# Sums of squares in column tiles of 32 tokens, routed sums kept transposed, and two of four squares on VectorE

## The chip, the cores and the metric

The kernel runs on one core of a Trainium2 chip. The metric is the device time of one execution in microseconds, as the median of several runs. TensorE (PE) multiplies, with its weight loads shown beside it as PEld; VectorE (DVE), ScalarE (ACT) and GpSimd (POOL) do the rest; SyncE (SP) issues the transfers.

## What is computed

A small vision tower of two layers over 64 images of 64 tokens, 256 wide. Layer 0 is a patch embedding, sparse attention and a mixture of experts; layer 1 is attention with a polynomial in place of the softmax, and a ternary feed-forward block with two norms. The parts that matter here, from the reference:

```python
att = polymax(where(causal, q @ k.T / 4, -inf))  # x>0: x*x+1; -100<=x<=0: 1-0.01*x; all over 1000
h = h + (att @ v) @ W_proj
# feed-forward of layer 1
x_norm = x / (rms(x) + EPS)
g = gelu(x_norm @ ternary(w_up).T)               # 256 -> 1024
h = h + (g / (rms(g) + EPS)) @ ternary(w_down).T # 1024 -> 256
```

The mean of the squares of g over its 1024 features is needed for each token. The routed part of layer 0's experts is computed for its nonzero rows: one-hot matrices send rows of a table through gates, and their sums over rows (an array of 64 slots by 128 hidden units) go through the experts' last matrix at the end.

## The kernel before, in words

512 tokens (8 images, 4 tiles of 128 tokens) make a slot, and there are 8 slots. A first half (up to 492 us) runs layer 0 for all slots. The second half, where the change lies, runs layer 1 slot by slot; VectorE, ScalarE and TensorE each go through their own list of work in a written order (the three functions `slot_B`), and semaphores join them. Slots 1 to 4 are trips of a loop and carry a batch of the routed rows each, slot 5 the last routed step, slots 6 and 7 none. Next to slot g's second half runs the first half of slot g + 1.

In a slot TensorE's order is: scores of tiles 2 and 3 (`B2_scores`, L623 and L629); the Gram products of the slot before (`gram`, L675); values of tiles 0 and 1 (L643); the downward products of the slot before for tiles 0 and 1 (`B3_down`, L687); a projection (L652); downward products of tiles 2 and 3; transposes (L322); the routed sums (`routed_sums`, L546) and the turn of the one-hots (L557); the keys and queries of the next slot (L332); values and projection of the other pair; routed gates (L567); the next slot's v (`B1_v`, L609); transposes; scores of the next slot's tiles 0 and 1; and the upward products (`B3_up`, L665).

An upward product of chunk f (of NF = 8 chunks of 128 features) fills a PSUM bank of 512 tokens. ScalarE takes it out through the gelu (L930, semaphore g_ok), makes a 16-bit high half of it (L932, gh_out), and VectorE subtracts to give the low half (`g_parts`, L1558, gl_out). Banks 4, 6, 7, 5 take turns, so that chunk f waits for the gelu of chunk f - 4. Between the gelus ScalarE does `relus` (L910), `quads` (the squares of the polynomial, L920) and `lins` (L915) of the next slot's tiles 0 and 1; `poly` on VectorE (L1501, L1507) waits for them.

The sum of squares of a token is the diagonal of a Gram matrix. `gram(g, f)` multiplies, for each tile of 128 tokens, the high half by the high and low halves: 4 matmuls of 128 by 128 weights and 256 columns for each f, collected over f in banks 6 and 7. All 8 chunks come after the scores of tile 3 (GRAM_LAG = NF). `mean_squares` on VectorE (L1565) multiplies each 128 by 256 block by a mask (1 on the diagonal of the first half, 2 on that of the second) and sums a row. The downward products use banks 6 and 7 too, and so wait for it (msq_ok). In the last slot `B3_down_last` alternates gram(f) and the 8 downward matmuls of f.

`routed_sums` multiplies 16 times 128 by 64 one-hot weights (f32) with 128 columns of gated rows, into 64 partitions; `sums_in` (L1439) adds them to racc. In slot 5 `gated_sums` multiplies racc by a transposed table, TensorE turns the product and ScalarE copies it out for `routed_out` (L579). The first slot's `quads` run on ScalarE while VectorE chooses the experts (`expert_choice`, which calls `first_polys` in the middle).

## Time and profile before

| | us |
|---|---|
| median of 3 runs | 953.96 (951.94 to 956.42) |
| the profiled execution | 949.92 |
| its span | 948.0 |
| TensorE busy | 775.9 (82% of the span) |
| VectorE busy | 655.9 (69%) |
| ScalarE busy | 390.5 (41%) |
| mean granted clock of TensorE | 0.916 |

The span is the time from the first to the last recorded instruction of the profiled execution; the rest of its 949.92 us lies around it. A granted clock of 1.0 is 2.4 GHz and 0.5 is 1.2 GHz. An engine that is busy for less than the whole span can still set the time of a stage, so the stages have to be read one by one. A matrix product in f32 leaves two pairs of records (weight load and matmul), one in f16 leaves one. Matmuls overlap: a record says 0.27 us where the next one begins 0.1 us later, so that paces are taken from start to start.

### The profile page before, as it was taken

Reading aid. Unit: us, or ns where it says so; the run is one execution under the profiler, and the core shown is the slowest. Engines: PE = TensorE matmul, PEld = TensorE weight load, DVE = VectorE, ACT = ScalarE, POOL = GpSimd, SP = SyncE. Lnnn points to the kernel's source line nnn. Section 1 sums busy time; section 2 is a strip of 40 time slices with the busy share of each in tenths; the row PEclk is TensorE's granted clock in tenths of the full one; section 3 lists DMA queues with packets and bytes.
Section 4 is the critical chain, followed back from the end, with each engine's and each line's share of the span. In section 5 each row is a group of like instructions: output and inputs, shape, how many; then the busy total and the mean of one; then the engine's idle time right before and its main releaser. Section 6 shows DMA issues by size and latency. Waiting matters only on the chain.

```text
span 948.0 us, 23223 instructions
## 1 busy us (share of the span) xinstructions
PE 775.9 (82%) x9703; PEld 544.6 (57%) x9703; DVE 655.9 (69%) x1471; ACT 390.5 (41%) x552; POOL 114.4 (12%) x76
## 2 busy tenths in 40 slices
PE   3669788897979788897678779999898989899956
PEld 2446465655546564655447448577575757575634
DVE  6457778586776858688768648596868678383742
ACT  3233332423333232333233274664839283554622
POOL 0030211312030031210001001010100001010000
PEclk9969999999999999998595689999999999998968
DMA  8051010201001010020000000000000000000000
GB/s 296 1 174 48 1 66 0 66 0 66 0 2 65 0 66 0 0 88 1 1 1 1 2 1 6 20 0 22 0 22 0 22 1 24 2 1 24 2 23 23
DMA packets 6779, 26.97 MB, mean 28 GB/s; under 512 B 2256, under 2 KB 3152, under 8 KB 5072
## 3 DMA queue, kind: packets, MB, share of 16 engines
q1 hardware_dynamic: 6736, 26.35, 7.5%
q8 instruction: 33, 0.54, 0.2%
q14 instruction: 10, 0.08, 0.0%
HBM read 22.15 MB, written 4.19 MB: 28 GB/s over the span
## 4 chain that ended last, share of the span: by engine, by line
PE 40%; issue 24%; DVE 22%; ACT 7%; POOL 6%; DMA 1%; DVEq 0%; POOLq 0%; SPq 0%; ACTq 0%
PE PS L304 8%; PE PS L687 5%; PE PS L332 5%; PE PS L652 3%; POOL w_s L1021 3%; PE PS L629 3%; PE PS L322 3%; DVE kM L1155 2%; PE PS L675 2%; PE PS L430 2%; PE PS L665 2%; PE PS L546 2%; DVE xn L1124 2%; PE PS L623 2%; POOL rstd L1005 2%
## 5 line engine op out<-in xcount | busy, mean ns | idle before, releaser
L304 PE MATMUL PS<-tokW_h,w_s 128*128 128x256 f16 x576 | 72.2, 289 | 27.0 <-DVE w_s L1299 16.4
L665 PE MATMUL PS<-xT,wqkv_h 128*128 128x512 f16 x256 | 70.8, 431 | 23.9 <-ACT w_s L930 22.1
L811 ACT ACTIVATE Pm<-Pm 128x1024 f32<-128x1024 f32 x32 | 33.9, 1058 | 135.5 <-DVE Pm L1225 135.5
L304 PEld LDWEIGHTS PS<-tokW_h,w_s 128*128 128x128 f16 x576 | 58.4, 103 | 38.1 <-issue 28.4
L1005 POOL TENSOR_TENSOR rstd<-ve,mhalf 128x4 f32<-128x4 f32 x24 | 28.0, 1168 | 363.1 <-DVE ve L1120 363.1
L1558 DVE TENSOR_TENSOR work<-w_s,work 128x512 f16<-128x512 f32 x48 | 32.5, 690 | 47.5 <-ACT work L932 47.5
L665 PEld LDWEIGHTS PS<-xT,wqkv_h 128*128 128x128 f16 x256 | 25.2, 107 | 64.5 <-ACT w_s L930 32.5
L322 PE MATMUL PS<-ident_s,xn 128*128 128x128 f32 x256 | 45.6, 303 | 15.6 <-DVE xn L1124 14.9
L818 ACT ACTIVATE PT<-PS 128x512 f32<-128x512 f32 x64 | 37.6, 595 | 44.0 <-PE PS L420 43.8
L332 PE MATMUL PS<-xT,wat_h 128*128 128x512 f16 x192 | 48.5, 415 | 7.6 <-DVE xT L1494 7.6
L1021 POOL TENSOR_TENSOR w_s<-work,w_s 128x1536 f16<-128x1536 f32 x14 | 43.1, 3102 | 94.0 <-ACT w_s L842 94.0
L687 PE MATMUL PS<-tokW_h,work 128*128 128x256 f16 x448 | 51.3, 273 | 0.5 <-DVE msq L1565 0.5
L420 PE MATMUL PS<-ident_s,Pm 128*128 128x128 f32 x256 | 44.7, 310 | 8.1 <-ACT Pm L811 4.6
L687 PEld LDWEIGHTS PS<-tokW_h,work 128*128 128x128 f16 x448 | 43.3, 98 | 7.0 <-DVE msq L1565 0.7
L1112 DVE BATCH_NORM_STATS2 st<-H 128x6 f32 (+1 forms) x128 | 45.6, 413 | 2.0 <-DVE H L1519 0.5
L430 PE MATMUL PS<-vbuf,PT 128*64 128x34 f32 x1024 | 42.7, 236 | 4.8 <-ACT PT L818 4.7
L322 PEld LDWEIGHTS PS<-ident_s,xn 128*128 128x128 f32 x256 | 31.3, 150 | 26.4 <-DVE xn L1124 17.2
L1124 DVE TENSOR_SCALAR xn<-H,mv,rstd 128x256 f32 (+1 forms) x96 | 33.1, 407 | 19.2 <-POOL rstd L1005 19.2
L1234 DVE RECIPROCAL rden<-PS 128x16 f32<-128x16 f32 x32 | 8.2, 256 | 55.1 <-PE PS L430 55.1
L430 PEld LDWEIGHTS PS<-vbuf,PT 128*64 128x64 f32 x1024 | 37.2, 149 | 14.9 <-ACT PT L818 7.7
L408 PE MATMUL PS<-mb,selb 128*128 128x256 bf16 x128 | 22.5, 305 | 26.7 <-DVE Pm L1225 20.3
L652 PE MATMUL PS<-wpr_s,xT 128*128 128x256 f32 x128 | 34.8, 419 | 11.2 <-DVE xT L1512 11.2
(237 smaller groups left out, 1672.8 us busy)
## 6 DMA issues: line engine op xcount, KB each, us to landing
work<-in_x SPq DMA_DIRECT2D x8, 1536.0 KB, 6.4
out<-H SPq DMA_DIRECT2D x8, 512.0 KB, 2.6
w_s<-in_w SPq DMA_DIRECT2D x3, 1024.0 KB, 6.8
wup_s<-in_wup SPq DMA_DIRECT2D x1, 1024.0 KB, 5.2
wdn_s<-in_wdn SPq DMA_DIRECT2D x1, 1024.0 KB, 7.2
w_s<-in_tokW SPq DMA_DIRECT2D x1, 768.0 KB, 7.5
wup_s<-in_wqkv SPq DMA_DIRECT2D x1, 768.0 KB, 8.1
wdn_s<-in_s SPq DMA_DIRECT2D x3, 256.0 KB, 6.1
```

The source lines that it names most:

```text
L304: m = pe.matmul(dst, halves_[xi][:, k, rows], w[:, wi, k, cols], start=(n == 0), stop=(n == 3 * chunks - 1))
L322: m = pe.transpose(PS[:, bank, t * P:(t + 1) * P], xn[:, t, c * P:(c + 1) * P], ident_s[:, :])
L332: m = pe.matmul(PS[0:cols, bank, :], w[:, wi, c, col:col + cols], x[xi][:, c, 0:TOK], start=(n == 0), stop=(n == 3 * C - 1))
L420: m = pe.transpose(PS[:, 4 + half, hp * P:(hp + 1) * P], Pm[:, t % 2, at:at + P], ident_s[:, :])
L430: m = pe.matmul(PS[b * L:(b + 1) * L, 6 + t % 2, hp * 2 * VW:(hp + 1) * 2 * VW], PT[:, t % 2, hp, b * L:(b + 1) * L], Vb[:, 2 * t + b, hp, ...
L652: m = pe.matmul(PS[:, bank, (t % 2) * E:(t % 2 + 1) * E], xT2[:, c, t * P:(t + 1) * P], wpr_s[:, c, :], start=(c == 0), stop=(c == C - 1))
L665: m = pe.matmul(PS[:, UP_BANKS[f % 4], :], wup_h[:, c, f * P:(f + 1) * P], part[:, c, :], start=(k == 0), stop=(k == 2 * C - 1))
L687: m = pe.matmul(PS[:, 6 + t // 2, (t % 2) * E:(t % 2 + 1) * E], part[:, f, t * P:(t + 1) * P], wdn_h[:, f, :], start=(k == 0), stop=(k == ...
L1005: pool.tensor_tensor(dst[:, :], src[:, :], mhalf[:, :], ALU.pow).then_inc(done, 1)
L1021: pool.tensor_tensor(p_lo[:, ks, :], patch[:, ks, :], p_hi[:, ks, :], ALU.subtract)\
L1112: dve.bn_stats(st_[:, t, :], H[:, TILES * g + t, :]).then_inc(in_st, 1)
L1124: dve.tensor_scalar(xn[:, t, :], H[:, TILES * g + t, :], mv_[:, t, 0:1], scale[:, t:t + 1], ALU.subtract, ALU.mult).then_inc(done, 1)
```

## The change

- `gram`: a tile of 128 tokens becomes four column tiles of 32 tokens. Each is a matmul with 32 columns of weights and 64 moving columns (32 high, 32 low), placed in its own 32 columns of the array; 16 matmuls for each f in place of 4, all collected in 256 columns of bank 6. The masks and the outputs of `mean_squares` shrink to 128 by 64, and it waits for one semaphore count a slot.
- GRAM_LAG becomes 4: the Gram products of chunks 0 to 3 are issued within `B3_up`, each after the upward product four chunks later; chunks 4 to 7 stay behind the scores.
- Bank 6 is no longer an upward bank: three banks (4, 7, 5) take turns, and chunk f waits for the gelu of chunk f - 3. The downward products of tiles 0 and 1 go to bank 7 and no longer wait for the mean squares; those of tiles 2 and 3 go to bank 6 and wait for all four. Queries swap banks 6 and 7.
- `quads` of tiles 0 and 1 leave ScalarE: VectorE multiplies (`v_quads`), ahead of `g_parts` in every slot and in `first_polys`. Those of tiles 2 and 3 stay on ScalarE.
- ScalarE issues the high half of chunk f behind the gelu of chunk f + 1 (and, for the first two, behind `lins`).
- `routed_sums` swaps its operands: weights are the 128 by 128 gated rows, the moving side the 64 one-hot columns; the result, and racc, are the transposed array of 128 by 64. `gated_sums` gives gT at once; one transpose and one copy go at the start (tabC), and another transpose with its copy in slot 5.

Left out of the diff below are renamed semaphores, the banks in `a_B1_q` and `ffn_out`, and the removed lines of `routed_tables`.

```diff
@@ -147,9 +147,9 @@
         PH = PS[:, 0:2, :].rearrange("p b n -> p (b n)").bitcast(F16)
-        racc = sb("racc", [64, HID]); gm = sb("gm", [64, HID]); gT = sb("gT", [P, 64])
-        UP_BANKS = (4, 6, 7, 5)
-        GRAM_LAG = NF
+        racc = sb("racc", [P, 64]); gT = sb("gT", [P, 64])
+        UP_BANKS = (4, 7, 5)
+        GRAM_LAG = 4
...
@@ -187,8 +187,8 @@
         lin = (u, late)
-        diag = PT[:, 0, 0:2, :].rearrange("p k n -> p (k n)")
-        diag_out = PT[:, 1, :, :].rearrange("p (t k) n -> p t (k n)", t=TILES)
+        diag = PT[:, 0, 0, 0:64]
+        diag_out = PT[:, 1, 0:TILES, 0:64]
...
@@ -543,7 +542,7 @@
                 for k in range(RB):
-                    m = pe.matmul(PS[0:64, 2, 0:HID], one_hot_w[:, k, :], wz_k[:, k, :],
+                    m = pe.matmul(PS[:, 2, 0:64], wz_k[:, k, :], one_hot_w[:, k, :],
...
@@ -572,8 +571,6 @@
-                pe.wait_ge(gm_ok, 1)
-                pe.transpose(PS[:, 0, 0:64], gm[:, :], ident_s[0:64, 0:64]).then_inc(gT_mm, 1)
...
@@ -590,9 +587,9 @@
                         pe.wait_ge(h5_ok, TILES * (g - 2) + 2 * c + 2)
-                    elif not first(g) and c == 1:
+                    elif not first(g) and c == 0:
                         pe.wait_ge(h4_ok, 1)
-                    proj_T(6 + c, wat_h, c * P, (x1_hi, x1_lo), Bq_mm)
+                    proj_T(7 - c, wat_h, c * P, (x1_hi, x1_lo), Bq_mm)
...
@@ -657,12 +654,12 @@
                 for f in range(NF):
-                    if f == 3 and nxt:
+                    if f == 2 and nxt:
                         pe.wait_ge(Bv_out, 4 * g + 8)
-                    if f >= 4:
-                        pe.wait_ge(g_ok, NF * g + f - 3)
+                    if f >= 3:
+                        pe.wait_ge(g_ok, NF * g + f - 2)
                     for k, (part, c) in enumerate((part, c) for part in (x4_hi, x4_lo) for c in range(C)):
-                        m = pe.matmul(PS[:, UP_BANKS[f % 4], :], wup_h[:, c, f * P:(f + 1) * P], part[:, c, :],
+                        m = pe.matmul(PS[:, UP_BANKS[f % 3], :], wup_h[:, c, f * P:(f + 1) * P], part[:, c, :],
...
@@ -672,19 +669,21 @@
                 for t in range(TILES):
-                    m = pe.matmul(PS[:, 6 + t // 2, (t % 2) * E:(t % 2 + 1) * E], G_hi[:, f, t * P:(t + 1) * P],
-                                  G_both[:, f, :, t * P:(t + 1) * P], start=(f == 0 and t % 2 == 0),
-                                  stop=(f == NF - 1), skip_group_check=True)
-                    if f == NF - 1 and t % 2:
-                        m.then_inc(ss_mm, 1)
+                    for i in range(4):
+                        at = t * P + 32 * i
+                        m = pe.matmul(PS[32 * i:32 * i + 32, 6, t * 64:(t + 1) * 64], G_hi[:, f, at:at + 32],
+                                      G_both[:, f, :, at:at + 32], start=(f == 0 and t == 0), stop=(f == NF - 1),
+                                      tile_position=(0, 32 * i), skip_group_check=True)
+                if f == NF - 1:
+                    m.then_inc(ss_mm, 1)
             def B3_down(g, tiles):
                 for t in tiles:
-                    if t % 2 == 0:
-                        pe.wait_ge(msq_ok, TILES * g + t + 2)
+                    if t == 2:
+                        pe.wait_ge(msq_ok, TILES * g + TILES)
                     for k, (part, f) in enumerate((part, f) for part in (G_hi, G_lo) for f in range(NF)):
-                        m = pe.matmul(PS[:, 6 + t // 2, (t % 2) * E:(t % 2 + 1) * E],
+                        m = pe.matmul(PS[:, 7 - t // 2, (t % 2) * E:(t % 2 + 1) * E],
...
@@ -694,7 +693,6 @@
                     if f >= NF - GRAM_LAG:
-                        pe.wait_ge(g_ok, NF * g + NF)
...
@@ -919,6 +917,10 @@
+            def g_high(g, f):
+                act.wait_ge(g_ok, NF * g + f + 1)
+                act.activation(G_hi[:, f, :], g32[f], ACT.Copy).then_inc(gh_out, 1)
+
...
@@ -927,12 +929,12 @@
                         act.wait_ge(gl_out, NF * g)
-                    act.activation(g32[f], PS[:, UP_BANKS[f % 4], :], ACT.Gelu).then_inc(g_ok, 1)
-                    act.wait_ge(g_ok, NF * g + f + 1)
-                    act.activation(G_hi[:, f, :], g32[f], ACT.Copy).then_inc(gh_out, 1)
+                    act.activation(g32[f], PS[:, UP_BANKS[f % 3], :], ACT.Gelu).then_inc(g_ok, 1)
                     if f < 2 and nxt:
-                        quads(g + 1, f)
                         lins(g + 1, f)
+                    if f > 0:
+                        g_high(g, f - 1)
+                g_high(g, NF - 1)
...
@@ -1468,8 +1465,9 @@
                 dve.wait_ge(racc_ok, LAST - 1)
-                dve.scalar_tensor_tensor(out=gm[:, :], in0=racc[:, :], scalar=0.5, in1=tabC[:, :], op0=ALU.mult,
-                                         op1=ALU.mult).then_inc(gm_ok, 1)
+                dve.wait_ge(tabT_ok, 2)
+                dve.scalar_tensor_tensor(out=gT[:, :], in0=racc[:, :], scalar=0.5, in1=AC[1][:, :], op0=ALU.mult,
+                                         op1=ALU.mult).then_inc(gT_ok, 1)
...
@@ -1497,7 +1495,10 @@
                 dve.wait_ge(lin_ok, TILES * g + t + 1)
-                dve.wait_ge(quad_ok, TILES * g + t + 1)
+                if t < 2:
+                    dve.wait_ge(quadv_ok, 2 * g + t + 1)
+                else:
+                    dve.wait_ge(quad_ok, 2 * g + t - 1)
...
@@ -1506,6 +1507,11 @@
                                          in1=relu_s[t % 2][:, :], op0=ALU.is_le, op1=ALU.mult).then_inc(f2_ok, 1)
+
+            def v_quads(g, t):
+                dve.wait_ge(relu_ok, TILES * g + t + 1)
+                v = relu_s[t % 2][:, :]
+                dve.tensor_tensor(v, v, v, ALU.mult).then_inc(quadv_ok, 1)
...
@@ -1561,8 +1567,8 @@
                 for t in range(TILES):
-                    dve.wait_ge(ss_mm, 2 * g + t // 2 + 1)
-                    dve.tensor_tensor_reduce(diag_out[:, t, :], PS[:, 6 + t // 2, (t % 2) * E:(t % 2 + 1) * E], diag,
+                    dve.wait_ge(ss_mm, g + 1)
+                    dve.tensor_tensor_reduce(diag_out[:, t, :], PS[:, 6, t * 64:(t + 1) * 64], diag,
...
@@ -1624,6 +1630,9 @@
                     weighted_hots(g)
+                if nxt:
+                    v_quads(g + 1, 0)
+                    v_quads(g + 1, 1)
...
@@ -1642,8 +1651,10 @@
             attend(LAST, 3)
-            for k in range(2):
-                dve.tensor_scalar(diag[:, k * P:(k + 1) * P], ident_s[:, :], 1.0 + k, None, ALU.mult).then_inc(diag_ok, 1)
+            dve.tensor_reduce(diag[:, 0:32], ident_s[:, :].rearrange("p (b j) -> p j b", j=32), AX.X, ALU.add)\
+               .then_inc(diag_ok, 1)
+            dve.wait_ge(diag_ok, 1)
+            dve.tensor_scalar(diag[:, 32:64], diag[:, 0:32], 2.0, None, ALU.mult).then_inc(diag_ok, 1)
...
@@ -1656,6 +1667,8 @@
             def first_polys():
+                v_quads(0, 0)
+                v_quads(0, 1)
                 poly(0, 0)
                 poly(0, 1)
```

## Rows read from the trace of the kernel before

**Rows 1.** The page, its sections 1 and 2: busy time, and the granted clock in 40 slices.
```profile
PE 775.9 (82%) x9703; PEld 544.6 (57%) x9703; DVE 655.9 (69%) x1471; ACT 390.5 (41%) x552; POOL 114.4 (12%) x76
...
PEclk9969999999999999998595689999999999998968
```
**Rows 2.** Windows: length, then busy us (instructions) of each engine, granted clock, DMA.
```profile
662.00:677.00 15.00, 11.16 (x117) 5.86 (x112) 11.00 (x13) 14.38 (x22) 0.00 (x0) 1.00 0.00 0
677.00:692.00 15.00, 14.50 (x179) 12.64 (x178) 14.32 (x39) 6.73 (x9) 3.17 (x3) 1.00 0.00 0
```
**Rows 3.** Timeline, up stage of one slot: start us, length us, engine, line, out<-in, count [idle before].
```profile
662.17 4.49 PE L665 MATMUL PS<-xT,wqkv_h 128*128 128x512 f16 x20
...
664.19 0.60 ACT L930 ACTIVATE w_s<-PS 128x512 f32<-128x512 f32 x1
664.82 0.63 ACT L932 ACTIVATE work<-w_s 128x512 f16<-128x512 f32 x1
665.36 1.04 ACT L920 ACTIVATE th<-th 128x1024 f32<-128x1024 f32 x1
665.49 0.69 DVE L1558 TENSOR_TENSOR work<-w_s,work 128x512 f16<-128x512 f32 x1 [1.12 <-ACT work L932]
...
670.86 2.19 PE L665 MATMUL PS<-xT,wqkv_h 128*128 128x512 f16 x8 [1.97 <-ACT w_s L930]
...
673.25 1.22 DVE L1501 SCALAR_TENSOR_TENSOR hs<-late,hs 128x1024 f32<-128x1024 f32 x1
```
**Rows 4.** Timeline, the same slot from its Gram products to the next product stage.
```profile
676.69 3.67 PE L675 MATMUL PS<-work 128*128 128x256 f16 x32 [0.56 <-ACT tokW_h L930]
...
677.46 0.69 DVE L1558 TENSOR_TENSOR work<-tokW_h,work 128x512 f16<-128x512 f32 x1
...
681.05 0.42 DVE L1565 CUSTOM_DVE_ANT_0 PT<-PS,PT 128x256 f32<-128x256 f32 x1
...
681.88 3.67 PE L687 MATMUL PS<-tokW_h,work 128*128 128x256 f16 x32 [0.50 <-DVE msq L1565]
...
691.57 3.47 PEld L546 LDWEIGHTS PS<-wup_s,wdn_s 128*64 128x64 f32 x32 [0.17 <-issue]
...
691.87 1.29 DVE L1494 TENSOR_TENSOR xT<-PS,xT 128x512 f16<-128x512 f32 x2
...
696.10 5.35 PE L332 MATMUL PS<-xT,wat_h 128*128 128x512 f16 x24
```
**Rows 5.** Timeline, weight loads of small matmuls, for their pace from start to start.
```profile
648.98 0.94 PEld L643 LDWEIGHTS PS<-Pm,vbuf 128*32 128x32 f32 x64 [0.42 <-issue]
...
654.71 2.71 PEld L609 LDWEIGHTS PS<-wat_h,xT 128*64 128x64 f16 x96
...
652.82 1.78 PEld L567 LDWEIGHTS PS<-tabA,w_s 64*128 64x128 f16 x32 [0.33 <-issue]
```
**Rows 6.** Windows of L527 alone (128x128 f32 weights, 8 columns): busy us (count), clock.
```profile
500.00:501.00 1.00, 1.00 (x11) 1.00 0.00 0
```
**Rows 7.** Timeline, the first slot, where VectorE chooses the experts.
```profile
505.95 1.23 DVE L1501 SCALAR_TENSOR_TENSOR th<-u,th 128x1024 f32<-128x1024 f32 x1
...
521.71 1.94 PE L643 MATMUL PS<-Pm,vbuf 128*32 128x64 f32 x64 [2.99 <-DVE racc L1427]
```
**Rows 8.** Timeline, the end of the last slot.
```profile
929.65 1.91 PE L701 MATMUL PS<-tokW_h,work 128*128 128x256 f16 x8
...
939.64 0.60 PE L675 MATMUL PS<-work 128*128 128x256 f16 x4
940.07 1.04 PE L701 MATMUL PS<-tokW_h,work 128*128 128x256 f16 x8
940.16 0.42 DVE L1565 CUSTOM_DVE_ANT_0 PT<-PS,PT 128x256 f32<-128x256 f32 x1 [10.03 <-PE PS L675]
```
**Rows 9.** Windows across an up stage, columns as in Rows 2.
```profile
622.00:723.00 101.00, 91.45 (x1255) 69.00 (x1252) 76.02 (x165) 58.75 (x80) 10.00 (x8) 1.00 0.03 10
723.00:728.00 5.00, 4.73 (x40) 2.26 (x41) 4.59 (x5) 4.84 (x10) 0.00 (x0) 0.66 0.00 0
```

More of the change, by code:

```diff
@@ L141, in build @@
         AC = [sb("AT", [P, 64]), sb("CT", [P, 64])]
-        tabA = sb("tabA", [64, 2, HID], F16); tabC = sb("tabC", [64, HID])
+        tabA = sb("tabA", [64, 2, HID], F16)
         one_hot = s1_h[:, :, :, :].rearrange("p k c n -> p (k c n)").rearrange("p (k e) -> p k e", k=RB)
@@ L529, in routed_tables @@
                     m.then_inc(tab_mm, 1)
-                for n in range(2):
-                    pe.wait_ge(tabT_ok, n + 1)
-                    pe.transpose(PS[0:64, 4 + 2 * n, 0:P], AC[n][:, :], ident_s[:, :]).then_inc(tab_t, 1)
+                pe.wait_ge(tabT_ok, 1)
+                pe.transpose(PS[0:64, 4, 0:P], AC[0][:, :], ident_s[:, :]).then_inc(tab_t, 1)
             def routed_count():
@@ L716, in slot_B @@
                     pe.wait_ge(Bv_out, 4 * g + 4)
-                    pe.wait_ge(tab_ok, 2)
+                    pe.wait_ge(tab_ok, 1)
+                    pe.wait_ge(tabT_ok, 2)
                     pe.wait_ge(tab_lo_ok, 1)
@@ L866, in routed_tables @@
                     act.activation(AC[n][:, :], PS[:, 4 + 2 * n, 0:64], ACT.Copy).then_inc(tabT_ok, 1)
-                for n, dst in enumerate((tabA[:, 0, :], tabC[:, :])):
-                    act.wait_ge(tab_t, n + 1)
-                    act.activation(dst, PS[0:64, 4 + 2 * n, 0:P], ACT.Copy).then_inc(tab_ok, 1)
+                act.wait_ge(tab_t, 1)
+                act.activation(tabA[:, 0, :], PS[0:64, 4, 0:P], ACT.Copy).then_inc(tab_ok, 1)
             def one_hot_turned(g):
@@ L948, in slot_B @@
                     a_B1_q(g + 1)
-                if routed == "last":
-                    act.wait_ge(gT_mm, 1)
-                    act.activation(gT[:, :], PS[:, 0, 0:64], ACT.Copy).then_inc(gT_ok, 1)
                 if nxt:
@@ L1438, in sums_in @@
                 dve.wait_ge(racc_ok, g)
-                dve.tensor_tensor(racc[:, :], racc[:, :], PS[0:64, 2, 0:HID], ALU.add).then_inc(racc_ok, 1)
+                dve.tensor_tensor(racc[:, :], racc[:, :], PS[:, 2, 0:64], ALU.add).then_inc(racc_ok, 1)
             def weighted(k, g):
@@ L1578, in ffn_out @@
                     at = TILES * g + t
-                    rows = PS[:, t, 0:E] if last else PS[:, 6 + t // 2, (t % 2) * E:(t % 2 + 1) * E]
+                    rows = PS[:, t, 0:E] if last else PS[:, 7 - t // 2, (t % 2) * E:(t % 2 + 1) * E]
                     dve.scalar_tensor_tensor(out=H[:, at, :], in0=rows, scalar=rgi[:, t:t + 1], in1=H[:, at, :],
```

6 lines of the change are left out of this document (2 added, 4 removed).

## The prediction

> **What bounds the kernel now.** I read the page first: TensorE is busy for 82% of the span, VectorE for 69%, ScalarE for 41%, and the granted clock is near full except at the seam of the two halves and in single slices [rows 1]. Shares over a whole span hide stages, so I then cut one slot of the second half into two stretches of 15 us. In the upward stretch ScalarE is busy for 14.38 us and TensorE for 11.16; in the next one TensorE has 14.50 and VectorE 14.32 [rows 2]. So a slot has a stage that ScalarE sets and one that TensorE sets, with VectorE close behind. The timeline says why. In the upward stage the first five chunks run without a break from 662.17; later ones wait for gelus, up to 1.97 us, because ScalarE puts squares of 1.04 us between them; the last chunk ends at 673.05 [rows 3]. Eight Gram products take 3.67 us from 676.69 on, and the downward products wait 0.50 us more for the mean squares and start at 681.88 [rows 4]. From there to 696.10 TensorE has no visible gap.
>
> **Price of a Gram product.** Before: 3.67 / 8 = 0.46 us for a chunk, all in TensorE's way [rows 4]. After: 16 small matmuls. No row shows accumulating f16 column tiles. The nearest row has the same tile form, 128 rows by 32 columns with 64 moving columns: L643 has 64 weight loads in 0.94 us, (0.94 - 0.11) / 63 = 13.2 ns from start to start, so 0.21 us for 16 [rows 5]. It is f32, where two records belong to one matmul of the program; if the pace belongs to the program's matmul, it is 26 ns, and L609 (f16, two column tiles, 128 moving columns) shows (2.71 - 0.11) / 95 = 27 ns [rows 5]. A floor below 0.21 isn't shown. If the column tiles did not overlap at all, L567 gives 55 ns (1.69 / 31), or 0.88 us for 16 [rows 5]. I take 0.21, the row of the same form and record, and keep 0.43 and 0.88 as ends.
>
> The row of L643 starts a record each 13.2 ns. The Trainium skill, "TensorE: Matmul & The Clock Gate", Part 1, says that matmuls never start closer than about 25 ns however few columns they have. By that figure the Gram products would hardly shrink (16 x 25 = 0.40 us); by the records it doesn't hold for column tiles. That is rival A below, which stands on the 26 and 27 ns of the rows alone.
>
> **Price of changing the tile form.** Before L643 the weight path idles for 0.42 us, before L567 for 0.33, part of which is the tail of the matmuls ahead [rows 5]. I take 0.2 us for each of the four trips into column tiles and back in the upward stage; bounds 0 and 0.4. The four chunks behind the scores share their form with the values that follow, which changed form before too: nothing. The Trainium skill, "TensorEngine Tiling (Array Packing)", Key Properties, says that a change of tiling mode drains the engine, which speaks against spreading Gram products among upward ones; no page gives its price.
>
> **The upward stage, step by step.** ScalarE is free at 664.19 [rows 3]. New order: gelu 0, lin 0, gelu 1, lin 1, high 0, then one gelu and one high half in turn. With paces of about 0.5 for a half-size instruction (664.82 to 665.36 is 0.54) and 0.91 for a full-size one (1.04 less an overlap of the same kind), high 0 begins at 664.19 + 2 x 0.5 + 2 x 0.91 = 667.0 and ends at 667.65, high 1 at 668.7. VectorE's two squares (1.23 us each, the price of L1501 [rows 7]) fit into its idle time before the first low half at 665.49 and up to the new one at 667.7: cost nothing, unless they slip past 667.7, then 1:1. Low 1 ends at 669.4; poly of tile 0 takes two instructions, to 671.8; low 2 ends at 672.45. Now TensorE: Gram 2 waits for it (queued behind it: chunk 7, Gram 3, both scores), so 672.5 + 0.41 + 0.9 + 0.41 = 674.2 against 673.05 minus the overlap, 672.9. The stage is longer by 1.3 us, although ScalarE is done about 1.4 us sooner (two squares of 1.04 less, a wait for chunk 7 more). The three banks cost about 0.4 us before chunk 4, hidden by the wait for Gram 0.
>
> **From there to the downward products.** The scores of two tiles take 3.2 (from 672.9 to 676.69 less the wait of 0.56 [rows 4]), so to 677.4. VectorE: low 3, poly of tile 1 to 675.4, four low halves to 677.9 (today 677.46 + 0.69 = 678.15 [rows 4]). Grams 4 to 7 are through at 678.2, values take 1.0 (0.94 [rows 5] and its rest), and the downward products start at 679.25 with no wait: 2.6 us sooner than 681.88 [rows 4]. Both mean squares and the turned values (VectorE, about 682) come before the projection needs them.
>
> **Routed sums.** Before, 32 records in 691.57 to 695.0, 107 ns each, bound by 128 moving f32 columns [rows 4]. After, 64 columns stream in half, but the weights are 128 wide: L527 with such weights and 8 columns has 11 records in a microsecond, 91 ns [rows 6]. 32 x (107 - 91) = 0.5 us saved; bounds 0 and 1.7 (half the pace). Beyond 0.6 of it VectorE's low halves of the next input, at 691.87 + 1.29 [rows 4], are what TensorE waits for.
>
> **The sum.** A slot with a batch (1 to 4): -2.6 - 0.5 = -3.1, four of them -12.4. Slot 5: no one-hot turn, so VectorE's chain comes last earlier, but a transpose, a copy and two handovers go: -2.7. Slot 6: no routed work, VectorE sets the time, which gains its earlier low halves (0.25) and four mean squares of a quarter of the columns (0.42 us record, say 0.11 less each; bounds 0 and 0.2): -0.7. Slot 7: VectorE waited for the Gram products, now hardly: -2.0. The end: the downward phase runs from 929.4 to 941.1 because 8 Gram products of 0.44 stand in it and the first two pairs are at half clock [rows 8]; four remain at 0.21 + 0.2, it starts about 1.9 us sooner, and the masks are shorter: -4.0. First slot: VectorE alone sets the time from the choice of experts to its reset of racc, for which TensorE waits 2.99 us, and two squares are put into it at 505.95: +2.5 [rows 7]. Tables and copies gone at the start are hidden behind that: 0. The extra clock loss: a low window in the upward stage (clock 0.66 over 5 us against 1.00 over 101 us [rows 9]) is half hidden today, since VectorE's last low half ends later than TensorE's scores; after it both end together, about 0.8 us in each of some four slots: +3. Sum -12.4 - 2.7 - 0.7 - 2.0 - 4.0 + 2.5 + 3 = -16.3. The profiled execution took 949.92, 4.0 below the median of 953.96, so 933.6 for it and 937.7 for the median; I give 938.
>
> **Rivals.**
> A. The matmuls go by 27 ns. For: L609, and that f32 records come in pairs. Against: each record of L643 has its own weight load. A Gram product costs 0.22 more, six of them in the path of a slot (two in the upward stage, four behind the scores), 1.3 us in seven slots, less where VectorE is last: +8, and +1 at the end: 947.
> B. Slower. Column tiles that accumulate in one bank don't overlap: 0.88 us a chunk, 0.67 more, x 6 x 7 slots = 28 plus 3 at the end: 969. It turns to a loss above 0.21 + 16 / 46 = 0.56 us a chunk, 35 ns a matmul. For: no row shows this form accumulating. Against: L643 writes four column tiles into one bank at 13.2 ns [rows 5].
> C. The clock. The upward stage has TensorE busy 8.2 of 12 us instead of 8.4 of 10.7, and low windows fall in such stages today [rows 9]. One more window of the 0.66 kind, (1 - 0.66) x 5 = 1.7 us of work lost, in each of seven slots: 950.
> D. The change does not bring TensorE's gain out: VectorE is last in every slot, as its chain is only 0.6 us behind after the change, and the gain of batch slots falls to that of slot 6: 4 x 2.4 = 10 less: 948.
>
> **Chances.** Forecast 0.56, A 0.15, B 0.06, C 0.11, D 0.07, the rest (squares that slow each other, a bank wait I have misread) 0.05. The measurement tells about 0.5% from no change, so faster means below 949.2: forecast, A, most of D and C: 0.81. Within 0.5%: half of C and rest: 0.11. Slower: B and rest: 0.08. Low end: changes of form at no cost (-3), sums at half price held by VectorE (-1), no clock loss (-3), a little at the seam: 929. High end takes in A, D and C: 951.
>
> **What would show it.** Column-tile weight loads with starts 13 ns apart or 27; the downward products starting 5.0 us behind the first score of tile 2, not 9.0 (672.9 to 681.88); TensorE waiting for the low half of chunk 2 (L1558) after poly; ScalarE idle before `relus` of tile 2; TensorE's routed sums at 91 ns; the first slot's values 2.5 us later. The forecast is wrong if the upward stage grows by more than 1.3 us, or if low windows come oftener.

## The result and the profile after

The changed kernel takes 927.8 us (median of 4 runs, 924.1 to 929.0) against 955.1 (951.9 to 956.4) for the kernel before: ratio 0.971, 95% interval 0.967 to 0.975. A second set of runs gave 929.1 and 0.973 (0.970 to 0.976). The forecast was 938 with a range from 929 to 951: the sign and most of the mechanism were right, but the gain is 25 to 27 us where 16 were forecast, and the time lies below the range. Among the experiments further down, one run of the kernel with filler (941.5 us) lay more than 1.5% above the fastest of that kernel and is left out of its median and ratio.

The page of the changed kernel, busy time and the granted clock in 40 slices, to be held against [rows 1]:

```profile
span 925.8 us, 24732 instructions
...
PE 752.7 (81%) x10469; PEld 525.1 (57%) x10469; DVE 666.5 (72%) x1487; ACT 368.6 (40%) x534; POOL 114.6 (12%) x76
...
PEclk9969999999999999999568579999999999999968
```

TensorE has 23 us less work although it runs 766 more matmuls; VectorE has 11 us more and ScalarE 22 less, most of it the squares: VectorE makes 16 of them in 18.9 us and saves 6.4 us on the shorter masks. The clock row shows full speed from the seam (the change from the first half to the second) to its last two slices.

Cut at two points, the start of the upward products and the start of the downward products, the third slot of the second half shows where its time went. Windows, first of the kernel before, then of the changed one; columns as in [rows 2]:

```profile
662.16:681.87 19.71, 15.39 (x204) 9.45 (x200) 15.67 (x29) 19.19 (x27) 1.84 (x1) 1.00 0.00 0
681.87:714.57 32.70, 31.53 (x432) 25.55 (x432) 24.09 (x57) 12.03 (x17) 3.16 (x4) 1.00 0.04 16
```

```profile
661.74:678.66 16.92, 13.64 (x300) 7.48 (x296) 15.40 (x21) 13.47 (x22) 0.00 (x0) 1.00 0.00 0
678.66:711.36 32.70, 31.54 (x439) 25.63 (x433) 25.57 (x68) 15.19 (x20) 4.99 (x4) 1.00 0.04 16
```

In the kernel before, the scores start at 672.88, 10.7 us after the first upward product:

```profile
672.88 0.60 PE L623 MATMUL PS<-cmaskb,identb 128*128 128x256 bf16 x4
```

The stretch from the downward products to the next upward ones takes 32.70 us in both. The slot's whole gain, 2.79 us, is in the stretch ahead of it: ScalarE was busy for 19.19 of 19.71 us there and is so for 13.47 of 16.92 now.

TensorE in that stretch of the changed kernel, from its timeline (start, length, idle time before), against [rows 3] and [rows 4]:

```profile
661.75 3.72 PE L662 MATMUL PS<-xT,wqkv_h 128*128 128x512 f16 x16
665.83 1.04 PE L662 MATMUL PS<-xT,wqkv_h 128*128 128x512 f16 x4 [0.37 <-ACT w_s L932]
667.98 0.30 PE L674 MATMUL PS<-work 128*32 128x64 f16 x16 [1.11 <-DVE work L1564]
...
672.06 0.30 PE L674 MATMUL PS<-work 128*32 128x64 f16 x16 [1.61 <-DVE work L1564]
...
673.75 0.61 PE L620 MATMUL PS<-cmaskb,identb 128*128 128x256 bf16 x4 [0.19 <-issue]
...
676.93 0.71 PEld L674 LDWEIGHTS PS<-work 128*32 128x32 f16 x64
...
678.67 3.67 PE L686 MATMUL PS<-tokW_h,work 128*128 128x256 f16 x32
```

VectorE in the same stretch:

```profile
665.00 1.22 DVE L1514 TENSOR_TENSOR hs<-hs 128x1024 f32<-128x1024 f32 x1
667.23 0.69 DVE L1564 TENSOR_TENSOR work<-w_s,work 128x512 f16<-128x512 f32 x1 [1.02 <-ACT work L922]
...
668.84 1.22 DVE L1502 SCALAR_TENSOR_TENSOR th<-u,th 128x1024 f32<-128x1024 f32 x1
...
676.73 0.68 DVE L1564 TENSOR_TENSOR work<-tokW_h,work 128x512 f16<-128x512 f32 x1
```

Gram products 0 and 2 wait for low halves, the second of them 1.61 us behind the polynomial (L1502, L1508). The last four take 0.71 us for 64 weight loads, and the downward products follow the values with no wait.

Interval by interval between starts of the upward products, changed kernel less before, beside the forecast (the first slot from its first matmul of L527 on, the end from the last slot's upward products on):

| part of the second half | forecast us | measured us |
|---|---|---|
| first slot, up to its upward products | +2.5 | +2.6 |
| the four slots with a batch | -12.4 | -12.8 (-4.1, -2.9, -2.8, -3.0) |
| slot 5 | -2.7 | -3.5 |
| slot 6 | -0.7 | -4.2 |
| slot 7 | -2.0 | -2.6 |
| end | -4.0 | -5.7 |
| clock | +3 | contained above |
| sum | -16.3 | -26.2 |

### The profile page after: what moved, and what is told of

Read it like the earlier page. It is cut to its first block, busy times and chain, and to the rows that moved or that the text cites. A ratio compares the mean times of both kernels' runs of the same rounds, so it can differ in the third digit from the quotient of the medians.

```text
span 925.8 us, 24732 instructions
## 1 busy us (share of the span) xinstructions
PE 752.7 (81%) x10469; PEld 525.1 (57%) x10469; DVE 666.5 (72%) x1487; ACT 368.6 (40%) x534; POOL 114.6 (12%) x76
## 4 chain that ended last, share of the span: by engine, by line
PE 36%; DVE 25%; issue 24%; ACT 6%; POOL 6%; DMA 1%; DVEq 0%; POOLq 0%; SPq 0%; ACTq 0%
PE PS L304 8%; PE PS L686 5%; PE PS L332 5%; PE PS L649 3%; POOL w_s L1018 3%; PE PS L322 3%; DVE kM L1152 2%; PE PS L626 2%; PE PS L430 2%; PE PS L545 2%; DVE xn L1121 2%; DVE work L1564 2%; PE PS L640 2%; ACT w_s L932 2%; POOL rstd L1002 2%
## 5 line engine op out<-in xcount | busy, mean ns | idle before, releaser
L662 PE MATMUL PS<-xT,wqkv_h 128*128 128x512 f16 x256 | 64.7, 390 | 5.4 <-ACT w_s L932 3.9
L662 PEld LDWEIGHTS PS<-xT,wqkv_h 128*128 128x128 f16 x256 | 21.8, 100 | 34.7 <-ACT w_s L932 10.3
```

The costliest lines, as they stand in the source:

```text
L662: m = pe.matmul(PS[:, UP_BANKS[f % 3], :], wup_h[:, c, f * P:(f + 1) * P], part[:, c, :], start=(k == 0), stop=(k == 2 * C - 1))
```

## The experiments

All ratios are to the kernel before, run on the same chip. "Up" is the stretch from the upward to the downward products of the third slot, "down" the one to the next upward products, both read from starts in each trace; a slot is their sum. "Inner" Gram products are those of chunks 0 to 3, which the changed kernel issues among the upward ones.

| kernel | time us | ratio (95%) | up | down |
|---|---|---|---|---|
| before | 952 to 955 | 1 | 19.71 | 32.70 |
| changed, again | 929.1 | 0.973 (0.970 to 0.976) | 16.9 | 32.7 |
| lag of 8 | 936.0 | 0.981 (0.977 to 0.985) | 17.77 | 33.26 |
| lag of 8 and filler | 932.4 (three runs) | 0.976 (0.970 to 0.982) | 16.92 | 32.70 |
| inner Gram products left out | 936.4 | 0.980 (0.976 to 0.983) | 17.78 | 33.25 |
| four squares on ScalarE | 944.3 | 0.991 (0.988 to 0.994) | 18.90 | 32.70 |
| first slot's squares on ScalarE | 923.5 | 0.970 (0.965 to 0.975) | 16.92 | 32.70 |
| and another order on ScalarE | 914.3 | 0.959 (0.957 to 0.961) | 15.42 | 32.70 |
| before, two squares on VectorE | 936.2 | 0.981 (0.979 to 0.983) | 18.30 | 32.70 |
| Gram products three times | 978.0 | 1.024 (1.022 to 1.027) | 25.9 | 32.7 |
| wide extra matmuls | 965.4 | 1.012 (1.008 to 1.016) | 26.1 | 32.7 |
| old order of the routed sums | 929.3 (one run) | | 16.92 | 32.70 |

**The changed kernel again.** No edit.

> The changed kernel once more, on the chip of the three runs beside it, to have its granted clock a second time. Both theories expect what was measured: 928 us (924 to 929), slots 49.6 us apart from one first downward product to the next, and no low clock between 546 and 888 us. If low windows are spread over the slots this time, the clock is chance and theory C (the Gram products within the upward stage hold the clock) loses its ground.

929.1 us, slots of 49.6 us; the low granted clock comes at the seam and then not before the last slot, as in the first profile.

**Gram products all behind the scores.**

```diff
-        GRAM_LAG = 4
+        GRAM_LAG = NF
```

> The changed kernel with all eight Gram products behind the scores, nothing else changed. In the stretch from upward stage to downward products VectorE's last low half comes last in either case, so the order alone should cost nothing in the slots and about 1.5 us in the last one. Theory C (Gram products among the upward ones hold the granted clock at 2.4 GHz): windows of low clock return in at least four of the eight upward stages, and the time is 932 to 935 us. Rival W (the clock holds because ScalarE's squares are gone and TensorE's waits are shorter): no low windows, 929 us.

936.0 us, 7 more than the changed kernel. Windows of this kernel around the end of the stretch "up" in its second slot (downward products from 632.04 on); the third number from the end of a line is the granted clock:

```profile
622.00:629.00 7.00, 5.55 (x174) 3.94 (x172) 6.84 (x9) 6.79 (x12) 0.00 (x0) 1.00 0.00 0
629.00:633.00 4.00, 3.47 (x114) 2.80 (x103) 3.96 (x15) 3.36 (x4) 1.18 (x1) 0.57 0.00 0
633.00:640.00 7.00, 7.00 (x59) 6.18 (x57) 6.81 (x20) 0.00 (x0) 1.79 (x2) 1.00 0.00 0
```

And the work that fell into it, one slot later:

```profile
681.06 1.91 PE L640 MATMUL PS<-Pm,vbuf 128*32 128x64 f32 x64
682.90 4.22 PE L686 MATMUL PS<-tokW_h,work 128*128 128x256 f16 x32
```

TensorE stands idle behind the scores for low halves (1.15 us and three times 0.3), the clock falls to half just then, and the values take 1.91 us in place of 1.10 and the downward products 4.22 in place of 3.67. That is nearly all of the 0.85 us more in "up" and the 0.56 in "down". It comes in every slot of this kernel and in none of the changed one's before the last.

**The same, with matmuls that fill.** Sixteen unused column-tile matmuls behind each of chunks 4 to 7.

```diff
-        GRAM_LAG = 4
+        GRAM_LAG = NF
...
+                    if f >= 4:
+                        for k in range(16):
+                            i, at = k % 4, P * (k // 4) + 32 * (k % 4)
+                            pe.matmul(PS[32 * i:32 * i + 32, 6, (k // 4) * 64:(k // 4 + 1) * 64],
+                                      x4_hi[:, 0, at:at + 32], x4_lo[:, 0, 64 * (k // 2):64 * (k // 2 + 1)],
+                                      start=(k == 0), stop=(k == 15),
+                                      tile_position=(0, 32 * i), skip_group_check=True)
```

> As the run before, and 16 column-tile matmuls of the same form that nobody uses stand behind each of the upward chunks 4 to 7, without a wait (extra work, the outputs stay the reference's). Theory C: the low windows go again, 929 to 930 us, although there is more to do than in the run before. Rival W: no low windows in either, and this one is the same or slower by up to 2 us (0.4 us each, hidden behind gelus).

In the trace the slots are 49.6 us again and the low clock is gone from the batch slots; work that nobody uses buys back 1.4 us a slot. By the runs the gain isn't settled: three of them lie at 924, 932 and 937.

**Four Gram products of eight left out** (those of chunks 0 to 3, so the mean squares are sums over half the columns).

```diff
                     if f >= GRAM_LAG:
-                        gram(g, f - GRAM_LAG)
```

> The changed kernel without the Gram products of chunks 0 to 3 in the upward stage, in all slots: the sum of squares is then that of half the features, so the output is not the reference's. Theory C: low windows return in at least four upward stages and the time does not fall, 927 to 932 us. Rival W: no low windows; TensorE no longer waits for the low half of chunk 2, VectorE still sets the start of the downward products, so 927 us. My price of a Gram product and of the change of tile form (0.16 + 0.3 us, four times a slot) shows as the upward stage being shorter by 1.3 to 3 us, without the slot being shorter.

936.4 us: doing less is 7 us slower. "Up" and "down" are those of the lag of 8 within 0.01 us, and the clock is the same:

```profile
629.00:633.00 4.00, 3.58 (x103) 2.98 (x104) 3.96 (x17) 3.17 (x4) 1.38 (x1) 0.57 0.00 0
```

So between these three kernels it isn't the amount of TensorE work that makes the difference in this stretch, but whether the clock holds, and with two squares on VectorE the small products among the upward ones hold it.

**The kernel before, profiled again.** No edit.

> The kernel before, unchanged, profiled a second time. The question is whether its first profile was a typical one: there the first upward product began at 554.6 us, while in the changed kernel and three variants of it, whose code up to the first slot's routed sums is the same, it began at 560.5 to 562.8, of which only 2.5 us are the two squares on VectorE. If the first profile was short in its first half by chance (and with it the forecast, which was made against that profile), a second one begins the first upward product at about 558.5 us and lasts about 953 us by the profile. If something in the changed kernel costs its first half 4 us, it begins again at 554.6 and lasts 950. Either way both theories expect the slots of the second half 52.3 to 53.5 us apart, with a low granted clock for 3.4 us in most of them.

953.2 us. First upward product in the first profile, then in this one:

```profile
554.59 1.68 PE L665 MATMUL PS<-xT,wqkv_h 128*128 128x512 f16 x7
```

```profile
558.22 2.12 PE L665 MATMUL PS<-xT,wqkv_h 128*128 128x512 f16 x9
```

The first profile was 3.6 us ahead by chance at the seam. The two profiles of before and after therefore differ by 22.2 us while the medians differ by 27.3; from the first upward product to the end the two profiles of before agree within 0.3 us (393.4 and 393.1), and the changed kernel takes 364.6.

**The four squares back on ScalarE.**

```diff
                     if f < 2 and nxt:
+                        quads(g + 1, f)
                         lins(g + 1, f)
...
-                if nxt:
-                    v_quads(g + 1, 0)
-                    v_quads(g + 1, 1)
```

> The changed kernel, but the squares of tiles 0 and 1 back on ScalarE in every slot, each between two GELUs as before. Theory S (ScalarE's queue sets when the low halves are done, so the two squares, 0.9 us each, stand on the path): the first slot gets back 2.5 us, and in each of the seven other slots ScalarE's chain of GELUs and high halves ends 1.8 us later and with it the low halves and the downward products, while VectorE, which has 2.4 us less, waits; 51.0 us a slot, and 7 x 1.5 - 2.5 = 8 us in sum: 936 us (932 to 941). Rival V (VectorE's queue sets them, and the two squares only fill it): the slots stay at 49.6 or fall to 48.5, and the time is 918 to 926 us.

944.3 us, 8 more than even theory S gave. Rival V falls: VectorE stands idle for 5.26 us until the first high half is there:

```profile
670.68 0.69 DVE L1564 TENSOR_TENSOR work<-w_s,work 128x512 f16<-128x512 f32 x1 [5.26 <-ACT work L922]
```

From one slot's first downward product to the next, the four batch intervals average 52.6 us where 51.0 were expected. The low clock is back in every slot, in the stretch where TensorE now waits for gelus (1.30 us) and low halves (2.06 us), although the inner Gram products are all there: they don't hold the clock by themselves. In the third slot, which the table shows, the low clock is not the reason of the longer "up": the first low half starts 7.46 us after the first upward product in place of 5.48, which is the 2.0 us, and what the clock costs vanishes in a shorter wait ahead of Gram product 2:

```profile
675.52 0.30 PE L674 MATMUL PS<-work 128*32 128x64 f16 x16 [0.35 <-DVE work L1564]
```

That wait was 1.61 us in the changed kernel. In the other three the low clock lasts 6.8 us in place of 3.4 and "up" is 0.9 to 1.8 us longer still; on average these two parts make the 3.0 us.

**Only the first slot's two squares on ScalarE.**

```diff
-            lins(0, 0)
-            lins(0, 1)
+            for t in range(2):
+                act.wait_ge(relu_ok, t + 1)
+                act.activation(relu_s[t][:, :], relu_s[t][:, :], ACT.Square).then_inc(quadv_ok, 1)
+                lins(0, t)
...
-                v_quads(0, 0)
-                v_quads(0, 1)
```

> The changed kernel, but the two squares of the first slot alone on ScalarE, as before, the other seven slots' on VectorE. In the changed kernel's trace VectorE makes them at 510.0 and 511.1 us, 1.22 us each, ahead of work that ends at 527.9 with TensorE waiting for it, and on ScalarE they had stood beside it. Theory (VectorE's queue sets the first slot's routed counts): -2.5 us, 925 to 926 us against 928 to 929. Rival (ScalarE's chain or the granted clock takes it back): the same as the changed kernel, 928 to 929. Slots of 49.6 us either way.

923.5 us with a scatter of 9, so the medians alone don't settle 2.5 us. The traces do: from the first matmul of L527 to the first upward product there are 55.55 us in the kernel before, 58.12 in the changed one and 55.46 here.

**Another order on ScalarE, on top of that.**

```diff
-                    if f < 2 and nxt:
-                        lins(g + 1, f)
-                    if f > 0:
+                    if f == 1:
+                        g_high(g, 0)
+                        g_high(g, 1)
+                        if nxt:
+                            lins(g + 1, 0)
+                    elif f == 2 and nxt:
+                        lins(g + 1, 1)
+                    elif f > 2:
                         g_high(g, f - 1)
```

> The version of e6_first_act with ScalarE's up stage in another order: gelu 0, gelu 1, high half 0, high half 1, lin 0, gelu 2, lin 1, high half 2 and so on, in place of gelu 0, lin 0, gelu 1, lin 1, high half 0. In the changed kernel VectorE stands idle until the first high half comes, and two Gram products wait 1.1 and 1.6 us for low halves that stand behind the polynomials. Theory: the first low halves come 2 us earlier, VectorE's queue no longer stands idle ahead of them, and the downward products start 1.0 to 1.5 us earlier in each of seven slots: 48.1 to 48.6 us a slot, 915 to 919 us. Rival 1 (the last GELU and high half, on ScalarE, set the end of the stage whatever VectorE does): 49.6 us a slot, 925 to 926 us as e6. Rival 2 (with the Gram products bunched earlier the granted clock falls in the slots again, at 1.4 us a slot): 934 us.

914.3 us, ratio 0.959: this kernel beats both. VectorE makes the low halves of chunks 0 and 1 before the first polynomial, without a gap, and a slot is 48.12 us. The two windows of its third slot:

```profile
652.28:667.70 15.42, 13.60 (x300) 7.58 (x296) 15.23 (x21) 13.36 (x22) 0.00 (x0) 1.00 0.00 0
667.70:700.40 32.70, 31.54 (x439) 25.65 (x432) 25.58 (x68) 15.18 (x20) 4.99 (x4) 1.00 0.04 16
```

VectorE is busy for 15.23 of 15.42 us: in that stretch it is the bound now. In the changed kernel it was busy for 15.40 of 16.92, and its gap ahead of the first low half went into the slot.

**The kernel before with two of the four squares on VectorE**, and nothing else of the change (the first slot's stay on ScalarE).

```diff
                     if f < 2 and nxt:
-                        quads(g + 1, f)
                         lins(g + 1, f)
...
+                if nxt:
+                    v_quads(g + 1, 0)
+                    v_quads(g + 1, 1)
```

> The kernel before with one part of the change alone: the squares of tiles 0 and 1 on VectorE in seven slots (the first slot's stay on ScalarE), the Gram products, their lag of eight chunks, the four banks and the routed sums as before. Undoing this part in the changed kernel cost 15.8 us by the medians. Theory A (the part is worth the same alone, as ScalarE set the upward stage): the slots fall from 52.4 to about 50 us and the time to 936 to 939 us. Rival J (the parts need each other: without Gram products among the upward ones, eight of them, 3.7 us, still stand between the scores and the downward products, behind low halves that now come no sooner, and the granted clock still falls in every slot): 51.3 to 52.2 us a slot, 945 to 951 us.

936.2 us: rival J falls. Its timeline between the scores and the downward products:

```profile
671.47 0.60 PE L623 MATMUL PS<-cmaskb,identb 128*128 128x256 bf16 x4
...
675.27 3.67 PE L675 MATMUL PS<-work 128*128 128x256 f16 x32 [0.56 <-ACT tokW_h L930]
...
680.95 1.26 PE L687 MATMUL PS<-tokW_h,work 128*128 128x256 f16 x10 [0.98 <-DVE msq L1572]
```

The scores start 8.82 us after the first upward product, not 10.72, and with the same eight Gram products behind them and a longer wait for the mean squares "up" is 18.30. The low clock, which the kernel before shows in most slots, doesn't come between 571 and 892 us. This part alone gives 17.7 us; all the rest of the change alone (the run with four squares on ScalarE) gives 10.1. Together, less the 2.5 us of the first slot, that is 25.3, and the change as a whole gives 25.0 to 27.3: the parts add up.

**Every Gram product three times.**

```diff
-                for t in range(TILES):
+                for n, t in ((n, t) for n in range(3) for t in range(TILES)):
...
-                                             1.0 / FF, 0.0, ALU.mult, ALU.add, msq[:, t:t + 1]).then_inc(msq_ok, 1)
+                                             1.0 / (3 * FF), 0.0, ALU.mult, ALU.add, msq[:, t:t + 1]).then_inc(msq_ok, 1)
```

> The changed kernel with every Gram product of a chunk made three times into the same sums (the mean squares divide by three times as many). A chunk then takes TensorE 0.50 us in place of 0.17, about what it took before. If six of eight stand in the path of a slot, as in my sum, a slot grows by 6 x 0.33 = 2.0 us to 51.6, and the time by 7 x 2.0 + 1.3 = 15 us to 943 (which says that the low price of a product was worth 15 us of the gain). Rival (VectorE's low halves and ScalarE set the slot, and TensorE has room): 49.6 to 50.3 us a slot, 928 to 934 us.

978.0 us, far outside both theories, so something else had begun to cost. TensorE stands idle with nothing that the profile shows as its reason (before this row it had last worked at 687.7):

```profile
691.08 0.61 PE L620 MATMUL PS<-cmaskb,identb 128*128 128x256 bf16 x4 [3.33 <-issue]
```

It also does so among the short products themselves and the values behind them, here behind the loop, in slot 6:

```profile
868.31 0.70 PE L674 MATMUL PS<-work 128*32 128x64 f16 x66 [1.85 <-issue]
...
872.04 0.27 PE L640 MATMUL PS<-Pm,vbuf 128*32 128x64 f32 x2 [2.11 <-issue]
```

**Wide matmuls in place of many.** Twelve instead of 32 extra ones for each chunk.

```diff
+                for k in range(12):
+                    i = k % 4
+                    m = pe.matmul(PS[32 * i:32 * i + 32, 6, 256:512], G_hi[:, f, 32 * k:32 * k + 32],
+                                  G_hi[:, f, 0:256], start=False, stop=(f == NF - 1),
+                                  tile_position=(0, 32 * i), skip_group_check=True)
```

> The changed kernel with 12 more column-tile matmuls of the same form behind the 16 of each chunk, each with 256 moving columns in place of 64, into an unused part of the bank; nothing of the result depends on them. If four column tiles of 256 columns run side by side they take 0.11 us a group, so 0.33 us a chunk, as much TensorE time as the 32 extra short matmuls of the run with every Gram product made three times, with 12 instructions in place of 32. That run came to 978 us where 943 was expected, with TensorE idle for up to 3.9 us a slot behind the short matmuls while nothing that the profile shows held it, and with its instruction queue moving 1.20 MB in place of 0.61. Theory I (it had run out of instructions): here those idle stretches are absent or much shorter, a slot is 51.0 to 51.8 us, and the time is 938 to 945 us. Rival L (any longer Gram product, whatever its instructions, costs that much, by the clock or by work that comes late): 970 us or more. Rival O (column tiles of 256 columns do not overlap: 1.3 us a chunk, 6 x 1.3 x 7 more): 980 or more, with TensorE busy and not idle.

965.4 us, between the theories, and the slots say why. Against the changed kernel the three intervals after the loop, each from one first downward product to the next, grew by 2.7, 1.8 and 1.8 us, near the 2.0 of six chunks at 0.33; with every product three times they grew by 5.2, 5.5 and 5.4, for about the same TensorE time in 32 instructions a chunk. Theory I holds there, and rivals L and O fall: the 12 matmuls of 256 columns have a row of 0.50 us, so column tiles do run side by side. But the three intervals within the loop grew by 8.3, 9.2 and 8.8. Each has one long wait, and always at the same place, ahead of the first matmul of the loop's body (L620):

```profile
689.72 1.03 PE L620 MATMUL PS<-cmaskb,identb 128*128 128x256 bf16 x4 [3.87 <-issue]
```

The instruction queue of the three pages, first the changed kernel's, then that of wide matmuls, then that of products made three times:

```profile
q8 instruction: 37, 0.61, 0.3%
```

```profile
q8 instruction: 67, 1.10, 0.5%
```

```profile
q8 instruction: 73, 1.20, 0.5%
```

From 630 to 690 us, inside the loop, neither the kernel before nor the changed one nor that with filler (64 more matmuls in the body) moves a packet of instructions, and the wide one moves nine, of 0.15 MB in all. So in the first three the loop's instructions stay where they are from turn to turn; with 96 more matmuls in the body they are loaded again, each of the three jumps back costs 3.6 to 4.2 us, and the scores behind it run at half clock (1.03 for 0.61 us). The Trainium skill, "Runtime: NRT & Kernel Launch", Instruction fetch mechanics, says that a taken branch whose target isn't held in the buffer forces a load before execution goes on; the trace agrees, with these waits.

**The old operand order of the routed sums** (the transposes that it needs at the end are left out, and with them the result of the routed part).

```diff
-                    m = pe.matmul(PS[:, 2, 0:64], wz_k[:, k, :], one_hot_w[:, k, :],
+                    m = pe.matmul(PS[0:64, 2, 0:HID], one_hot_w[:, k, :], wz_k[:, k, :],
```

> The changed kernel with the old operand order in the routed sums (64-column weights, 128 moving columns); the transposes that this order needs at the end are left out, and the result of the routed part with it. In the changed kernel the 32 matmuls take 3.72 us, in the kernel before 3.44. Theory (they stand in TensorE's path, and the new order is the slower one): the four intervals of slots with a batch fall from 49.61 to 49.33 us, 927.5 us by the profile if its first half is alike. Rival (VectorE sets that stretch): they stay at 49.6.

The slots stay at 49.6. Old order, then new order, each with the start of what follows:

```profile
639.97 3.71 PE L545 MATMUL PS<-wup_s,wdn_s 128*64 128x128 f32 x32
643.52 1.06 PE L556 MATMUL PS<-identh,s_h 128*64 128x128 f16 x16
```

```profile
638.65 3.68 PE L545 MATMUL PS<-wdn_s,wup_s 128*128 128x64 f32 x32
642.26 1.08 PE L556 MATMUL PS<-identh,s_h 128*64 128x128 f16 x16
```

3.55 us and 3.61 us from start to start: half the moving columns with twice the weight columns buy nothing and cost 2 ns a record. My expectation had compared lengths of weight-load rows, 3.72 against 3.44, which don't span the same thing; starts are what counts.

## Why the prediction came out as it did

**Right.** The stretch up to the downward products was forecast 2.6 us shorter and is 2.79 shorter: the upward part grew by 1.3 us (scores 12.0 us after the first upward product, before 10.7), Gram product 2 waits behind the polynomial, and the downward products start 4.9 us after the scores, 5.0 forecast, 9.0 before. The first slot's +2.5 measured +2.6, and putting its squares back recovers it. VectorE's squares fit into idle time. All four rivals fell: no slower pace, no loss of overlap, fewer low-clock windows and not more, and all batch slots gain.

**The price of a Gram product was too high, not too low.** I took 13.2 ns from L643 [rows 5], whose records are those of f32. The f16 products measure (0.71 - 0.10) / 63 = 9.7 ns. The 27 ns of L609, rival A, was the wrong row. At 16 a chunk the difference is 0.06 us, six times a slot: it can cover the 0.19 us by which the stretch beat its forecast. The Trainium skill, "TensorE: Matmul & The Clock Gate", Part 1, has 25 ns as the least distance of two matmuls; the trace disagrees for column tiles, with 9.7 ns.

**The clock term had the wrong sign.** This is the step that failed most. I took it that the low windows of the upward stages [rows 9] stay and will hit TensorE's path, and added 3 us for "the extra clock loss". The changed kernel has none from its first upward products to the last slot. Had they stayed, the price would even have been too low: with a lag of 8 they cost 1.4 us a slot, where I had 0.8. And the kernel before had losses that I had not looked for outside a batch slot. One is in the scores of slot 7's tiles 0 and 1, ahead of slot 6's upward products, in the kernel before and then in the changed one:

```profile
866.30 0.60 PE L623 MATMUL PS<-cmaskb,identb 128*128 128x256 bf16 x4
...
869.28 1.99 PE L629 MATMUL PS<-qT,kM 32*128 32x64 f32 x32
871.20 1.03 PE L665 MATMUL PS<-xT,wqkv_h 128*128 128x512 f16 x2
```

```profile
854.08 0.60 PE L620 MATMUL PS<-cmaskb,identb 128*128 128x256 bf16 x4
...
856.21 1.12 PE L626 MATMUL PS<-qT,kM 32*128 32x64 f32 x32
857.26 1.04 PE L662 MATMUL PS<-xT,wqkv_h 128*128 128x512 f16 x4
```

These two tiles of scores cost 4.90 us before and 3.18 after: 1.7 us of slot 6's gain. The first batch slot gained 4.1 where its neighbours gained 2.9, with the clock low from 563.6 to 570.4 us before; I put the difference, 1.2 us, down to it. At the end the first Gram and downward products of before run at half clock ([rows 8] has the eight of 1.91 us between these two rows):

```profile
928.85 1.01 PE L675 MATMUL PS<-work 128*128 128x256 f16 x4 [2.15 <-DVE work L1558]
...
932.21 1.04 PE L701 MATMUL PS<-tokW_h,work 128*128 128x256 f16 x8
```

From the one to the other are 3.36 us, where the same pieces take 1.74 later, and those of the changed kernel don't run at half clock: 1.6 us. Together 4.5 us gained where 3 were charged, so 7.5 of the 9.9 us by which the sum missed. I had asked only what a low window would cost in the new order, not whether the new order would still cause one. The three runs with a lag of 8, with filler and with products left out show that in the changed kernel the windows of the batch slots come without the inner Gram products or filler and not with them. The run with four squares on ScalarE shows that these products aren't enough when the waits grow, and the run of before with two squares moved that they are not the only way: there the windows are gone with the shorter waits for gelus (1.02 us for 1.97). What exactly makes the clock fall stays open.

**Slot 6 was read wrongly.** I had VectorE setting its time and gave it 0.7 us. Its downward products start 2.5 us earlier relative to its upward ones, like those of every other slot, and all of it arrives: 1.8 us more than forecast. VectorE was idle there for 2.1 to 2.3 us at a time, behind values and projections of TensorE, as rows of the kernel before show; I had taken its share of busy time for its place in the chain.

```profile
858.11 0.69 DVE L1512 TENSOR_SCALAR xT<-PS 128x512 f32<-128x512 f32 x1 [2.26 <-PE PS L643]
860.89 0.69 DVE L1519 TENSOR_TENSOR H<-H,PS 128x512 f32<-128x512 f32 x1 [2.09 <-PE PS L652]
```

**The routed sums gave nothing** where 0.5 us a slot was forecast, 2 in sum. The 91 ns of [rows 6] were taken with 8 moving columns; with 64 the pace is 113 ns, and the old order's, read from starts, is 111 and not 107. My lower bound, 0, was the answer. Without the clock the batch slots so gave 11.6 us where 12.4 were forecast, while slots 5 and 7 and the end gave 0.8, 0.6 and 0.1 more; these small terms nearly cancel, which is luck.

**Which part carried the gain** wasn't asked in the prediction, and it should have been. I costed the squares inside "the upward stage" and gave the heading, the price and two of four rivals to the Gram products. Alone, the squares are worth 17.7 us, and everything else 10.1. [rows 2] had said it: ScalarE busy for 14.38 of 15 us.

## What to carry to other kernels

Cut a repeated stage at two starts on the bound engine and compare the pieces between kernels: in the third slot one piece was 32.70 us in ten of twelve kernels, and nearly everything that mattered was in the other, where an edit was worth most when it relieved the engine that was busy for 97% of it. Ask of a change to the waits of TensorE whether it removes or makes low-clock windows, in every slot and not only in the one studied; in the changed kernel small products among the upward ones were worth 1.4 us a slot, more than their own time. When the bound has moved, look at what the next engine waits for: another order of ScalarE's instructions, so that VectorE never stood idle, gave another 1.5 us a slot.

## What the runs showed of the hardware

- Accumulating f16 column tiles (128 rows, 32 columns, 64 moving) start every 9.7 ns. Those with 256 moving columns run side by side: twelve have a row of 0.50 us, where f16 matmuls of 256 columns over the whole array start every 0.11 us.
- With f32 weights of 128 by 128 and 64 moving columns a record (two belong to one matmul of the program) starts every 113 ns, with 64 columns of weights and 128 moving ones 111, and with weights of 128 by 128 and 8 moving ones 91: swapping the sides to halve the moving one gains nothing.
- Coming out of column tiles costs little: 0.19 us of idle time between the last inner Gram product and the scores, where 0.2 was estimated.
- A loop's body has a size at which its instructions no longer stay on the engine. The changed kernel is below it, and so is the one with filler, with 64 more matmuls in the body; 96 more are above: 3.6 to 4.2 us at every jump back, and the scores behind it at half clock.
- In the straight code behind the loop the 32 short matmuls more for each chunk cost 5.4 us a slot, where 12 wide ones of about the same TensorE time cost about 2. With the short ones TensorE stands idle for 1.0 to 2.2 us at a time with no reason that the profile shows, with the wide ones for 0.8 at most. That it waits for instructions there fits, and isn't shown.
